# Post-norm decoder layer: DMA crossbar transposes in place of TensorE transposes for the two normalised activations

## What is computed

```
def _layernorm(x, eps=1e-05): return (x - mean(x)) / sqrt(var(x) + eps)
x1 = _layernorm(x  + softmax(q k^T * 256**-0.5) v @ Wo + bo)          # q, k, v = split(x @ Wqkv + bqkv), 256 columns each
x2 = _layernorm(x1 + softmax((x1 Wq^T + bq)(ctx Wk^T + bk)^T / 32) @ ctx)
x3 = _layernorm(x2 + (silu(x2 @ Wg) * (x2 @ Wu)) @ Wd)               # Wg, Wu: 1024x2752, Wd: 2752x1024, GPTQ 4 bits
```

## Time and profile before

| | |
|---|---|
| median of 3 runs | 1975.22 us (1974.12 to 1978.18) |
| profiled execution, its own time | 1978.52 us |
| its span | 1976.8 us |
| PE busy | 1889.8 us, 96% |
| DVE, ACT, POOL busy | 880.5, 476.2, 320.3 us |
| self-attention, set-up, cross-attention, weights | to 230, 390, 741, 1977 us |
| DMA issues of an x1 row block, of a Wq slab | 448 KB in 4.0 us, 512 KB in 4.4 us from issue to landing |

### The profile page before, as it was taken

How to read it: one execution, slowest core, us unless ns; L and a number is a source line. 1 busy time by engine, 2 the same in 40 slices (tenths; PEclk the granted TensorE clock), 3 DMA queues, 4 the chain that set the end, 5 groups by cost and what they waited for, 6 DMA issues and landing times.

```text
span 1976.8 us, 28966 instructions
## 1 busy us (share of the span) xinstructions
PE 1889.8 (96%) x11238; PEld 1094.2 (55%) x11238; DVE 880.5 (45%) x1404; ACT 476.2 (24%) x788; POOL 320.3 (16%) x262
## 2 busy tenths in 40 slices
PE   4898999899999987999999999999999999999998
PEld 2666644688888863544544444444455444444443
DVE  5578512578878865344344434434434311111111
ACT  2221102566556542212122222222121200000000
POOL 0221285111111102111112111111111000000000
PEclk9999999999999988999999999999999999999999
DMA  9232441234344311212121122121121322221220
GB/s 304 82 107 69 115 136 57 75 104 134 120 120 132 119 54 35 54 39 43 39 53 43 34 58 43 34 58 34 43 52 35 84 102 90 101 101 52 99 101 21
DMA packets 142336, 157.07 MB, mean 79 GB/s; under 512 B 101817, under 2 KB 116345, under 8 KB 140093
## 3 DMA queue, kind: packets, MB, share of 16 engines
q1 hardware_dynamic: 135772, 152.07, 26.5%
q10 hardware_dynamic: 6496, 4.06, 0.8%
HBM read 112.64 MB, written 43.46 MB: 79 GB/s over the span
## 4 chain that ended last, share of the span: by engine, by line
PE 57%; issue 32%; DVE 6%; POOL 2%; ACT 1%; DMA 1%; POOLq 0%; SPq 0%; DVEq 0%; ACTq 0%
PE psum L1303 54%; POOL arena L1024 1%; DMA arena<-in_x 1%; PE psum L1457 1%; PE psum L1574 1%; PE psum L1296 1%; PE psum L1592 1%; DVE arena L834 1%; POOL small L950 0%; DVE small L401 0%; DVE arena L394 0%; DVE arena L482 0%; DVE arena L714 0%; POOL arena L959 0%; DVE small L376 0%
## 5 line engine op out<-in xcount | busy, mean ns | idle before, releaser
L1303 PE MATMUL psum<-arena 128*128 128x448 f16 (+9 forms) x9432 | 1751.9, 347 | 26.3 <-POOL arena L1024 6.5
L1303 PEld LDWEIGHTS psum<-arena 128*128 128x128 f16 (+5 forms) x9432 | 972.5, 106 | 781.1 <-issue 96.6
L1049 POOL TENSOR_TENSOR arena<-arena 128x1024 f16<-128x1024 f32 (+1 forms) x65 | 139.1, 2140 | 685.9 <-ACT arena L1246 685.9
L890 DVE SCALAR_TENSOR_TENSOR arena<-psum,small,arena 128x448 f32<-128x448 f32 x84 | 57.4, 684 | 418.3 <-PE psum L1303 418.3
L930 DVE SCALAR_TENSOR_TENSOR arena<-psum,small,arena 128x512 f32<-128x512 f32 x28 | 21.0, 751 | 333.2 <-PE psum L1303 321.5
L1246 ACT ACTIVATE arena<-arena 128x1024 f16<-128x1024 f32 (+1 forms) x65 | 68.7, 1057 | 270.4 <-DVE arena L876 270.4
L950 POOL TENSOR_TENSOR small<-small 112x1 f32<-112x1 f32 (+1 forms) x46 | 25.5, 554 | 614.0 <-DVE small L381 613.9
L1259 ACT ACTIVATE arena<-arena 128x448 f16<-128x448 f32 (+1 forms) x88 | 50.7, 576 | 291.9 <-DVE arena L890 291.9
L1149 ACT ACTIVATE arena<-psum 128x750 f16<-128x750 f16 x96 | 72.0, 809 | 64.4 <-PE psum L1457 64.4
L874 DVE TENSOR_TENSOR arena<-arena,psum 128x1024 f32<-128x1024 uint32 x65 | 79.4, 1221 | 2.6
L896 DVE TENSOR_TENSOR arena<-arena 128x448 f16<-128x448 f32 (+1 forms) x88 | 55.0, 625 | 57.1 <-ACT arena L1259 57.1
(11 more groups left out here) (187 smaller groups left out, 878.3 us busy)
## 6 DMA issues: line engine op xcount, KB each, us to landing
h_scratch<-arena SPq DMA_DIRECT2D x88, 224.0 KB, 2.9
arena<-h_scratch SPq DMA_DIRECT2D x13, 1408.0 KB, 6.1
arena<-in_ctx SPq DMA_DIRECT2D x32, 512.0 KB, 3.6
arena<-in_x SPq DMA_DIRECT2D x32, 448.0 KB, 5.5
x_scratch<-arena SPq DMA_DIRECT2D x32, 448.0 KB, 3.1
arena<-x_scratch SPq DMA_DIRECT2D x30, 448.0 KB, 4.0
arena<-in_L_ffn_down_qweight SPq DMA_DIRECT2D x21, 512.0 KB
arena<-in_ctx SPq DMA_DIRECT2D x16, 448.0 KB
```

The costliest lines, as they stand in the source:

```text
L890: dve.scalar_tensor_tensor(h_f[0:n, :], up[0:n, :], sc_u[0:n, :], g_act[0:n, :], ALU.mult, ALU.mult).then_inc(s_hf, 1)
L1049: pool.tensor_tensor(dst[1], src, dst[0], ALU.subtract).then_inc(s_wl, 1)
L1303: mm = pe.matmul(out, a, r, start=(k == 0), stop=(k == len(pairs) - 1))
```

## The change

x1 and x2 are no longer transposed on PE. Their rows are split into high and low parts while they stand as rows in `yo` (112 rows on the partitions, 1024 columns), by ACT (`x1_hi`, `x2_hi`) and DVE (`x1_lo`, `x2_lo`). The x1 parts are stored by SP in a new HBM scratch `x1p_d` (448 KB a batch) and read back by a transposing DMA into `xtp`. The x2 parts stay in SBUF (`x2p`, two slots) and a transposing DMA from SBUF to SBUF writes them to `x2t`; for these the columns are reordered in the split, so that it reads the rows with a step of eight elements. The x1 split moves from the set-up and cross-attention into self-attention; the last batch of a group is split within the next group. All x1 row reloads for transposing go. The norm and split of batch 15 move behind the dequantisation of chunk 0's gate and up weights, and PE waits for the last x2 columns before block 3 of chunk 0 only. The diff, cut to its core:

```diff
@@ vector
+            def x1_lo(n, b):
+                dve.wait_ge(s_x1h, n + 1)
+                dve.scalar_tensor_tensor(x1p[0:S, b % 2, 1, :], yo[0:S, b % 2, :], XS, x1p[0:S, b % 2, 0, :],
+                                         ALU.mult, ALU.subtract).then_inc(s_x1l, 1)
...
@@ self_attention
                     x_max(g + 1)
                 if known(g, 1):
                     wo_split()
+                else:
+                    x1_lo(g * GB - 1, GB - 1)
...
                     norm_stats(yo[0:S, b % 2, :], n, s_y, 2 * n + 1)
+                    if b:
+                        x1_lo(n - 1, b - 1)
                     norm_apply(yo[0:S, b % 2, :], n, s_n)
...
@@ cross_attention
+            def x2_lo(n, b):
+                dve.wait_ge(s_hi, n + 1)
+                dve.scalar_tensor_tensor(x2p[0:S, b % 2, 1, :].rearrange("p (c q) -> p c q", c=KC),
+                                         yo[0:S, b % 2, :].rearrange("p (q c) -> p c q", c=KC), XS,
+                                         x2p[0:S, b % 2, 0, :].rearrange("p (c q) -> p c q", c=KC),
+                                         ALU.mult, ALU.subtract).then_inc(s_lo, 1)
...
                         context_max(n + 2, 2)
+                    if not known(n, 1):
+                        x2_lo(n - 1, b + 1)
                     add_attended(n, b)
...
-                    if more:
-                        x1t_lo(n + GB, b, 6)
-                    if not known(n, 1):
-                        x2t_lo(n - 1)
...
-            normalise(NB - 1, (NB - 1) % 2)
             dequant(0, 0, 0, 0)
-            x2t_lo(NB - 1)
             dequant(1, 1, 0, 0)
+            normalise(NB - 1, (NB - 1) % 2)
+            x2_lo(NB - 1, 1)
@@ gpsimd
-            inverse_std(2 * NB - 1, S)
...
             for m in range(2):
                 low_part(m, [wgu[0][m][:, l, :, :] for l in range(2)], m)
+            inverse_std(2 * NB - 1, S)
@@ scalar
+            def x1_hi(n, b, filled):
+                act.wait_ge(s_n, n + 1)
+                act.wait_ge(s_x1o[b % 2], 16 * filled)
+                act.activation(x1p[0:S, b % 2, 0, :], yo[0:S, b % 2, :], ACT.Identity, scale=XS).then_inc(s_x1h, 1)
...
                     act.activation(qkt[:, f, :], bk[2 + f % 2][:, 0:TG], ACT.Identity, scale=kq,
                                    bias=bqk[:, f:f + 1]).then_inc(s_qke, 1)
+                    if f == 0 and not known(g, 1):
+                        x1_hi(g * GB - 1, GB - 1, 2 * g)
...
+                for b in range(GB - 1):
+                    x1_hi(g * GB + b, b, 2 * g + b // 2 + 1)
...
+            def x2_hi(n, b, filled):
+                act.wait_ge(s_n, NB + n + 1)
+                act.wait_ge(s_x2t[b % 2], 16 * filled)
+                act.activation(x2p[0:S, b % 2, 0, :].rearrange("p (c q) -> p c q", c=KC),
+                               yo[0:S, b % 2, :].rearrange("p (q c) -> p c q", c=KC), ACT.Identity,
+                               scale=XS).then_inc(s_hi, 1)
...
                     probs_hi(n)
+                    if not known(n, 1):
+                        x2_hi(n - 1, b + 1, 2 * g + (b + 1) // 2)
                     if has(1):
                         context_t(n + 1, CT_ACT[5:])
...
+            x1_hi(NB - 1, GB - 1, NB // 2)
             with act.Fori(0, KC // 2 - 1) as e:
...
-            x1t_hi(0, 0, 4)
-            x1t_hi(1, 1, 6)
-            for m in (2, 3):
-                act.dma_start(xs3[0:S, m % 2, :], x1_d[m * S:(m + 1) * S, :]).then_inc(s_xs3[m % 2], 16)
...
             for m in range(2):
                 high_part(m, wgu[0][m][:, 0, :, :], m)
+            x2_hi(NB - 1, 1, NB // 2)
@@ tensor
             for i in range(2):
-                if i:
-                    pe.wait_ge(s_x1l, 4)
-                x1_transposed(2 * i, 2 * i, 4)
-                if i == 0:
-                    pe.wait_ge(s_cf, 1)
-                x1_transposed(2 * i + 1, 2 * i + 1, 6)
                 m_chunk(KC // 2 - 1, i)
...
                     logits(n, b)
-                    if not known(n, 1):
-                        pe.wait_ge(s_x1l, 2 * (n + GB) if more else 2 * NB)
+                    if has(2) and b % 2 == 0:
+                        pe.wait_ge(s_x1t[1 - b // 2], 32 * (g + 1 + b // 2))
...
-                    if more:
-                        pe.wait_ge(s_y3, 2 * (n + 1))
-                        x1_transposed(n + GB, b, 6)
-                    if not known(n, 1):
-                        if not known(n, 2):
-                            pe.wait_ge(s_lo, 2 * (n - 1) + 1)
-                        x2_transposed(n - 1, (b + 1) % 2)
...
@@ chunk
+                    if t == 3:
+                        for k in range(2):
+                            pe.wait_ge(s_x2t[k], 16 * (NB // 2 + 1))
...
             gather_gu(0, 0, 0, 0)
-            pe.wait_ge(s_lo, 2 * (NB - 1) + 1)
-            x2_transposed(NB - 1, 1)
             gather_gu(1, 1, 0, 0)
-            pe.wait_ge(s_lo, 2 * NB + 1)
+            for i in range(2):
+                pe.wait_ge(s_x2t[i], 16 * (NB // 2 - 1))
@@ sync
+            def store_parts(n, s):
+                sp.wait_ge(s_x1l, n + 1)
+                sp.dma_start(rows(x1p_d, n), x1p[0:S, s, :, :].rearrange("p l d -> p (l d)")).then_inc(s_x1o[s], 16)
+            def load_x1t(m, b):
+                sp.dma_start_transpose(xtp.rearrange("p l k t -> p (l k) t")[:, :, b * S:(b + 1) * S],
+                                       rows(x1p_d, m)).then_inc(s_x1t[b // 2], 16)
...
                     sp.dma_start(rows(x1_d, g * GB + b), yo[0:S, b % 2, :]).then_inc(s_yout[b % 2], 16)
+                    if b or not known(g, 1):
+                        store_parts(g * GB + b - 1, (b + 1) % 2)
...
+            for i in range(2):
+                sp.wait_ge(s_x1o[i], 16 * (GB // 2 + 1))
+            sp.wait_ge(s_v, 2 * NG)
+            for m in range(GB):
+                load_x1t(m, m)
             self_attention(NG - 1, False, False)
...
+            def load_x2t(n, s):
+                sp.wait_ge(s_lo, n + 1)
+                sp.dma_start_transpose(x2t.rearrange("p l k t -> p (l k) t")[:, :, bass.ds(n * S, S)],
+                                       x2p[0:S, s, :, :].rearrange("p l d -> p (l d)")).then_inc(s_x2t[s], 16)
             def cross_attention(g, loop):
                 for b in range(GB):
                     n = g * GB + b
+                    if loop and b % 2 == 0:
+                        sp.wait_ge(s_g, KC + 4 * n)
+                        for k in range(2):
+                            load_x1t(n + GB + k, b + k)
...
+                    if not known(n, 1):
+                        load_x2t(n - 1, (b + 1) % 2)
...
-                    if loop or n + 6 < NB:
-                        sp.wait_ge(s_x1t, 2 * n + 10)
-                        load_rows(n + 6, (b + 2) % GB)
```

More of the change, by code:

```diff
@@ L478, in self_attention @@
                     dve.wait_ge(s_yout[b % 2], 16 * (2 * g + b // 2 + 1))
+                    if not known(n, 2):
+                        dve.wait_ge(s_x1l, n - 1)
                     for h in range(2):
@@ L1379, in _ @@
             pe.wait_ge(s_wk, 48)
-            def x1_transposed(m, b, bank):
-                pe.wait_ge(s_xs3[b % 2], 8 * (m - b % 2) + 16)
-                for j in range(2):
-                    for a in range(4):
-                        mm = pe.transpose(bk[bank + j][:, a * S:(a + 1) * S],
-                                          xs3[0:S, b % 2, (4 * j + a) * P:(4 * j + a + 1) * P], ident[0:S, 0:S])
-                    mm.then_inc(s_x1t, 1)
             def m_chunk(e, i):
@@ L1446, in context_t @@
                         pe.wait_ge(s_y3, 2 * (n - 1))
-                    if c == 0 and not known(n, 2):
-                        pe.wait_ge(s_lo, 2 * (n - 1) - 1)
                     if c in (4, 5, 6, 7):
@@ L1767, in next_ctx @@
                     load_ctx(n, c)
-            for m in range(2):
-                load_rows(m, m)
             next_ctx(0)
+            store_parts(NB - 1, (NB - 1) % 2)
             sp.wait_ge(s_t, T["sel"])
@@ L1777, in _ @@
             sp.dma_start(tab_d[64:64 + GD, :], dtab_d[3 * GD:, :]).then_inc(s_tin[2], 16)
+            for i in range(2):
+                sp.wait_ge(s_x1o[i], 16 * (NB // 2 + 1))
             for n in range(2):
```

90 lines of the change are left out of this document (26 added, 64 removed).

## The result

The changed kernel is slower: 1984.31 us (median of 5 runs, 1983.2 to 1985.66) against 1974.12 us of the kernel before on the same chip, a ratio of 1.0042 with a 95% interval of 1.003 to 1.0054. The forecast was 1961.2 us with a range of 1953 to 1980: wrong in sign, and outside the range. The profiled execution took 1983.89 us with a span of 1982.2, 5.4 us over the span of before.

A forecast was written before the change was run, and what follows sets the result against it. TensorE, busy 96% of the span, was taken as the bound. Set-up -3.1, cross-attention -0.8, -7.0, -0.5, loop edge -3.1, hand-over -4.45 and self-attention +5.0 gave -14.0 us: 1961.2 us against 1975.2, range 1953 to 1980.

The forecast's parts named there:

- Transposes in cross-attention, and PE's idle time: Cross-attention: removed transposes save 1.66 us once a pair, plus a 0.27 us wait; after odd batches the 4.93 us chain stays.
- a lost clock: Cross-attention rival: PE's idle after odd batches brings the lower clock each time, so nothing is saved; chance 0.02.
- The x2 high part on ACT: Cross-attention: 1.15 us ahead of the last context evacuation delays the attended product by 0.25 us a batch.
- The forecast's own sign of being wrong: Stated in advance: wrong if ACT's strided split in cross-attention is over 1.5 us.
- no penalty: ACT's x2 split: a strided read costs nothing extra, taken from DVE's L577 at about 0.95 ns an element.
- strided reads cost: Rival, x2 split in cross-attention: ACT's part takes 1.7 us, giving 1968, or 2.3 us, giving 1976; chance 0.20.
- Loop edge: Cross-attention batch 8, second loop turn: PE arrives 1.66 us earlier; 1.4 and the clock's 1.66 come back, -3.1 us.
- Self-attention: Groups 1 to 3: PE waits for ACT's late x1 high part, low parts mostly hidden; +5.0 us, from 3.1 to 7.3.
- Set-up: Before cross-attention: both x1 transpose sets and the DVE and ACT work on them go, -3.1 us.
- Transposing DMAs: 32 transfers of 448 KB for x1 and x2: 2 us each, covered, cost 0.
- the slow rival: Set-up and cross-attention: transposing DMAs of 7.3 us each give 1988; counts above 4.5, breaks even near 6.5; chance 0.20.
- Hand-over and weights: After the last sum: dequantisation starts sooner, -4.45 us, with norm and split hidden beside the first chunk; weights stage untouched.

The follow-up runs named there:

- Run 4: Changed kernel plus 16 unread identity transposes where PE idles before the logits of each even batch: 1979.8 us, ratio 1.0027 to the kernel before.
- run 1: Also `x2_late`: changed kernel with ACT's x2 high part moved behind the last context evacuation; 1968.44 us, ratio 0.9964 to the kernel before.
- Run 7: Changed kernel with DVE's x1 low part replaced by a maximum over the same rows, one SBUF operand: 1980.01 us, ratio 1.0032.
- run 5: Changed kernel with ACT's x1 high parts of batches 2 and 3 put behind the next group's q/k evacuations 1 and 2: 1984.71 us, ratio 1.006.
- `x2_contiguous`: Changed kernel with both x2 splits reading and writing in order, which gives another output: 1971.7 us, ratio 0.998.
- `combo`: Changed kernel with ACT's x2 and x1 high parts later, x1 low part before the statistics, x1 parts stored earlier: 1982.79 us, ratio 1.0045.
- `late_apply`: On run 1: x1 low part behind the norm's last step, ACT's x1 high parts behind q/k evacuations 1 and 2; 1965.83 us, ratio 0.9951.
- the two with filler: 16 unread transposes in PE's idle time before even logits, added to the changed kernel (1979.8 us) and to run 1 (1965.44 us).

## Why the prediction was wrong

*Transposes in cross-attention, and PE's idle time (right as arithmetic, wrong on the clock).* The 4.93 us chain after odd batches stayed to the hundredth, and PE idles 2.2 to 2.4 us in it, as forecast. The step that failed is "PE already goes 2.4 us without products there at full clock", by which a lost clock got 0.02. Before, 1.66 us of this time were transposes and only 0.6 to 0.7 was idle; it had gone without products, but not without work. Run 4 shows the difference: with transposes put back, idle time is 0.5 to 0.6 us and the clock is full in seven of seven even batches, without them in three of seven. 4 times 1.67 = 6.7 us. The Trainium skill, TensorE: Matmul & The Clock Gate, What's actually happening, says that the clock is set by how busy PE has been recently; the rows of the two kernels agree (8.02 us after 2.2 to 2.4 us of idle time in four of seven batches, 6.35 after 0.5 to 0.6 in all).

*The x2 high part on ACT (right place, wrong size).* The term was 0.25 us a batch at 1.15 us. It measured 2.07, and the waits come to 1.0 to 1.2 us in 13 batches, 14.4 us in all, and 3.3 where batch 14 waited 1.65 before: 11.2 + 1.6 = 12.8 us over the forecast. The forecast's own sign of being wrong, a split over 1.5 us, came true. The failed step is the reading of L577 as "no penalty". It set the 0.95 ns an element of the strided row against nothing; the same operation in order stands right behind it in the trace of before:

```profile
217.67 0.94 DVE L579 TENSOR_SCALAR arena<-arena,small 128x2752 bf16<-128x2752 bf16 x1
```

Less the 273 ns of one column, that is 0.24 ns an element, a quarter of L577's (which has one arithmetic step more). The norm, float32 in order and with as many arithmetic steps as L577, takes 0.81 us for 1024 elements, 0.53 ns each. So the row spoke for a price, and the rival "strided reads cost" had the mechanism, and its far end (2.3 us) the size; it fell short since it counted neither the clock nor the lock. The Trainium skill's rule on Memory Cachelines (Advanced Engine Details and Errata), which the forecast set aside, held in direction: a read that takes every element from another line cost 1.94 times on ACT and 1.64 times on DVE. With the ACT part hidden (run 1) the whole stage is 337.7 us, against 338.7 in the forecast; two clock losses (+3.3) and no ACT delay (-3.25) are in it and cancel, so the other terms were right to 1 us there and to 2.5 in the changed kernel. Part of the 2.5 is arithmetic: two x2 sets of 0.89, less ACT's 0.25 in two to four batches, are 0.8 to 1.3 us for batches 12 to 15, not 0.5.

*Loop edge.* The 2.03 us of "issue" are gone, and batch 8 starts 4.93 us after the max transpose, as forecast. The clock's 1.66 did not come back: batch 8 is one of the four.

*Self-attention.* The forecast's 5.0 had PE stall at product 3 for ACT, and the low parts "hidden by POOL waits except 0.7". The second is what failed, in group 1, which loses 6.2 us where 1.1 to 2.5 were forecast. POOL's pow, on which the norm waits, reads SBUF too and cannot run beside a DVE instruction with two SBUF operands, so the low part is in the chain in full, and at times stands behind POOL's 2.35 us add as well. Run 7 puts this lock at 4.0 us, of which 1.7 is the lower clock after PE's 4.54 us wait (after 1.35 us in run 7 the granted clock is 1.00); without the lock the stage loses 4.65, near the 5.0. Group 2 was forecast to lose 2 to 3.4 and lost nothing, and that two misses partly cancel there is luck. The norm's 2.83 us beside an add in the trace of before was a sign of the lock that the forecast passed over. The stall at ACT is real (9.7 us of waits), but run 5 shows that it was not the bound: taken away, PE waits for DVE. The forecast also missed that the high part of batch 2 stands in front of evacuation 0.

*Set-up.* 2.0 of 3.1 us. The four transposing DMAs hold SP for 7.8 us (233.96 to 241.75), and PE waits 0.91 for a Wq slab. That these cause the wait was not tried.

*Transposing DMAs.* 4.0 and 4.9 us to landing, neither 2 nor 1.8; under the 6.5 at which the slow rival broke even, though in the set-up above the 4.5 from which it was to count; what was found there is the 0.91. No product waits for one in cross-attention, so cost 0 holds there, and the rival that came nearest in time (1988) did so for a reason that isn't there.

*Hand-over and weights.* -5.5 for -4.45; the cover held. The first 48 products of chunk 0 take 10.76 us instead of 12.18, which was not counted, and make the last 1.3 us.

The misses together: 12.8 (ACT) + 6.7 (clock) + 3.7 (self-attention, the lock above all) + 1.1 (set-up) - 1.1 - 1.3, less the 2.5 by which the other terms of cross-attention were too small, are the 19.4 us. That is the miss between the profiles' spans; between the medians of the two kernels it is 24.2, and no profile says to which stage the other 4.8 belong. What stays open besides is how self-attention could take the split without the lock; three orders of it gave nothing that the ratios or the start of the set-up can tell.

## What to carry to other kernels

Before an instruction is moved to DVE, look at what POOL runs at that time, whether DVE's instruction takes two large SBUF operands, and how long DVE's other instructions already take beside POOL's: one short POOL instruction in a chain makes "hidden" work visible. Before a row is read as "no penalty", find the same operation in order and compare the time of one element. When work is taken off TensorE in a place where it waits anyway, look at the granted clock of the stretch after it, and count the idle time that is left, not the time saved. A new instruction on ACT goes behind whatever TensorE waits for next; here that one move turned a change slower by 0.42% into one faster by 0.36%.

## What the runs showed of the hardware

- A float32 read of 112x1024 with a step of 32 bytes: 2.07 us on ACT (1.07 in order), 2.00 on DVE (1.22). A float16 write with a step of 256 bytes: 4.76 and, with a float16 read of the same step, 4.72 us. A bfloat16 `tensor_scalar` on DVE: 0.95 ns an element with a step of 16 bytes, 0.24 in order.
- DVE and POOL took turns by whole instructions: 1.22 us became 3.16, 0.81 became 2.84, 0.55 became 1.53. A maximum over one SBUF operand (1.21 us) and a DVE instruction on PSUM and one large SBUF operand (0.75) kept their time beside POOL's add; the norm, with one large SBUF operand, did not (2.83 and 2.84 for 0.81).
- In five of the kernels (the changed one, `x2_late`, `x2_contiguous`, `combo`, `late_apply`) idle time of 1.83 or 1.84 us before even logits was never followed by the lower clock (0 of 12), idle time of 2.03 to 2.4 us in 17 of 23 cases, and 0.3 to 0.7 never (the kernel before and the two with filler). Why some of the 23 kept the full clock was not found.
- A transposing DMA of 448 KB took 4.0 us from SBUF and 4.9 us from HBM to landing, and 1.5 to 2.2 us of SP's queue each.
